# The first token tiles of a quantized feed-forward kernel, shared between two issuing queues

## What is computed

```python
hidden = jnp.concatenate([cond, cond], axis=-1)
x_mean = jnp.mean(x, axis=1, keepdims=True)
fused = jnp.concatenate([x, x_mean * ones_L, hidden[:, None, :] * ones_L], axis=-1)
relation = jax.nn.relu(jnp.einsum('bld,do->blo', fused, W) + b)

def quant_linear(x, w, b):
    xq, s_in = quant_act_uint8(x)                # one scale: max(x)/255
    wq, s_w = quant_weight_int8_perchannel(w)    # a scale for each row of w
    bq = quant_bias_int32(b, s_in, s_w)
    return jnp.einsum('btd,fd->btf', xq, wq) + bq

h = jax.nn.relu(quant_linear(relation, w1, b1))
return x + quant_linear(h, w2, b2)
```

## Time and profile before

| | before |
|---|---|
| median of the timed runs | 329.53 us (329.33 to 330.42, 3 runs) |
| the profiled execution | 330.61 us, span on the core 328.8 us |
| TensorE matmul busy | 318.3 us, 97% of the span |
| VectorE busy | 266.8 us, 81% |
| ScalarE busy | 208.9 us, 64% |
| GpSimd busy | 76.0 us, 23% |
| DMA | 75.27 MB, mean 229 GB/s |

### The profile page before, as it was taken

One profiled execution on the slowest core, in us unless ns is written; L12 is line 12 of the kernel. 1 busy time (PEld: TensorE's weight loads), 2 busy tenths in 40 slices (PEclk: granted clock), 3 DMA queues, 4 the chain that ended last, 5 costly groups with the idle time before them and its releaser, 6 DMA issues. The chain is left out here.

```text
span 328.8 us, 4649 instructions
## 1 busy us (share of the span) xinstructions
PE 318.3 (97%) x1508; PEld 181.8 (55%) x1508; DVE 266.8 (81%) x586; ACT 208.9 (64%) x335; POOL 76.0 (23%) x60
## 2 busy tenths in 40 slices
PE   6999999999999999989999999789999999999996
PEld 6888888888775544344444444334444444444444
DVE  1549988987985899999999998885759577595996
ACT  2423865587386999656666665089875958759700
POOL 1005336643500388993280000000000000000000
PEclk9999999999999999999999999999999999999999
DMA  7959999999973888747770160379953799766316
GB/s 223 272 162 255 231 166 235 251 230 359 282 153 64 81 334 335 291 173 319 324 321 0 36 222 0 127 274 388 429 203 119 275 418 426 286 237 222 143 39 255
DMA packets 49382, 75.27 MB, mean 229 GB/s; under 512 B 19768, under 2 KB 32336, under 8 KB 44624
## 3 DMA queue, kind: packets, MB, share of 16 engines
q1 hardware_dynamic: 49168, 74.72, 72.8%
q10 hardware_dynamic: 192, 0.28, 0.4%
HBM read 45.63 MB, written 25.17 MB: 215 GB/s over the span
## 5 line engine op out<-in xcount | busy, mean ns | idle before, releaser
L833 ACT ACTIVATE steps<-hidden,s_quant 128x512 int16 (+1 forms) x124 | 76.8, 710 | 21.1 <-DVE w_t L1123 11.2
L705 PE MATMUL bank<-w_t 128*128 128x512 f16 x256 | 56.3, 379 | 0.9 <-DVE w_t L1158 0.9
L1027 DVE TENSOR_SCALAR_CACHE_REDUCE hidden<-bank,qb,hmax 128x512 f32<-128x512 f32 x59 | 45.4, 807 | 5.2 <-PE bank L595 4.6
L467 PE MATMUL bank<-x_hi,cw_hi 128*128 128x512 f32 x128 | 48.3, 393 | 0.3 <-ACT x_hi L735 0.3
L467 PE MATMUL bank<-x_lo,cw_hi 128*128 128x512 f32 x128 | 48.5, 390 | 0.0
L467 PE MATMUL bank<-x_hi,cw_lo 128*128 128x512 f32 x128 | 48.4, 389 | 0.0
L1046 DVE CUSTOM_DVE_ANT_0 hidden<-hidden,bank,hmax 128x512 f32<-128x512 f32 x69 | 47.9, 742 | 0.0
L403 POOL TENSOR_TENSOR x_lo<-hidden,x_hi 128x512 fp32r<-128x512 f32 x24 | 30.4, 1300 | 54.1 <-ACT x_hi L735 54.1
L705 PEld LDWEIGHTS bank<-w_t 128*128 128x128 f16 x256 | 24.8, 98 | 31.9 <-DVE w_t L1158 1.5
L705 PE MATMUL bank<-w_t,pool_q 128*128 128x512 f16 x192 | 41.9, 379 | 0.0
L595 PE MATMUL bank<-pool_r,pool_q 128*128 128x512 f16 x152 | 38.2, 379 | 0.0
(11 more groups left out here) (132 smaller groups left out, 421.6 us busy)
## 6 DMA issues: line engine op xcount, KB each, us to landing
hidden_spill<-hidden SPq DMA_DIRECT2D x16, 1024.0 KB, 4.3
hidden<-hidden_spill SPq DMA_DIRECT2D x16, 1024.0 KB, 8.3
pool_r<-in_x_dram SPq DMA_DIRECT2D x8, 1024.0 KB, 5.3
x_in<-in_x_dram SPq DMA_DIRECT2D x28, 256.0 KB, 5.7
pool_q<-in_L_ffn_w_dram SPq DMA_DIRECT2D x7, 1024.0 KB, 9.1
out_dram<-pool_r SPq DMA_DIRECT2D x7, 1024.0 KB, 4.8
pool_r<-in_L_cond_W_dram SPq DMA_DIRECT2D x2, 1024.0 KB, 10.8
x_in<-in_x_dram SPq DMA_DIRECT2D x1, 1024.0 KB, 9.5
```

Of the source, the lines that this page charges most:

```text
L467: return pe.matmul(REL[ot][:, :], w[:, k, ot * P:(ot + 1) * P], v[:, n % 2, k, :], start=(k == 0 and w is cw_hi and v is x_hi), stop=(k == ...
L705: mm = pe.matmul(bank[TJ * par + j][:, :], hid_q[par][:, ft, j * P:(j + 1) * P], w2_t[:, ft, :], start=(ft == 0), stop=(ft == FT - 1))
L833: ins = act.activation(steps[:, q % 2, f, :], hidden[:, bass.ds(slot * HB + ft * TB, TB)], ACT.Copy, scale=s_quant[:, ft:ft + 1])
L1027: dve.tensor_scalar(hidden[:, at:at + TB], y_bank[:, :], qb1[:, ft:ft + 1], hmax[:, ft:ft + 1], ALU.add, ALU.max, accum_out=hmax[:, ft:ft ...
```

## The change

SyncE's queue issues token tiles 0 and 2 of block 0 only. ScalarE's queue issues tile 1, then weight chunk 0, then tile 3, then the three small tables as before. Destinations, sizes, semaphores and all waits stay as they are.

```diff
@@ block.sync
-            for j in range(TJ):
+            for j in range(0, TJ, 2):
                 sp.dma_start(x_in[:, 0, j * D:(j + 1) * D], x_blocks[0, :, j, :]).then_inc(x0_landed[j], 16)
             for k in range(1, KD):
                 sp.dma_start(cw_in[:, k, :], cw_turned[0, :, k, :]).then_inc(cw_landed[k], 16)
@@ block.scalar
+            act.dma_start(x_in[:, 0, D:2 * D], x_blocks[0, :, 1, :]).then_inc(x0_landed[1], 16)
             act.dma_start(cw_in[:, 0, :], cw_turned[0, :, 0, :]).then_inc(cw_landed[0], 16)
+            act.dma_start(x_in[:, 0, 3 * D:4 * D], x_blocks[0, :, 3, :]).then_inc(x0_landed[3], 16)
             act.dma_start(cond_rows, cond.rearrange("b (k p) -> b k p", p=P)).then_inc(rows_landed, 16)
```

## The result

The change makes the kernel slower: 330.53 us median (330.10 to 333.81, 19 runs) against 329.33 us (329.08 to 330.48, 19 runs); the ratio is 1.0047, 95% interval 1.0032 to 1.0063. That is +1.2 us at the medians, where -0.1 us was forecast. The time lies inside the forecast's range (328.5 to 330.9); its direction is the opposite one.

The account below looks back on a forecast made before the run. TensorE was taken as the bound from the first relation product on, so only the start mattered. Tile 1's wait going gave -0.12 us, all else 0: 329.53 - 0.12 = 329.4 us, range 328.5 to 330.9.

Parts of the forecast that it names:

- TensorE is thus the bound from the first relation product on: From the first relation product at 10.63 us TensorE has no slack; moving that product moves the end by the same amount.
- Tile 0: change 0: Token tile 0, still SyncE's first issue at 0.75 us, lands at 5.6 us as before; at most 0.74 us to gain.
- tile 0 comes sooner: Rival, faster: sharing with another piece of x brings tile 0 early, gaining at most 0.86 us, 328.7 us; chance 0.11.
- Tile 3 takes the slot of weight chunk 1, 9.0: Worst case for token tile 3 at the start: it lands at 9.0 us instead of 8.2.
- Wanted at 9.11: hidden by 0.1 us: TensorE wants token tile 3 at 9.11 us, so landing at 9.0 costs nothing, with 0.1 us to spare.
- The sum: Whole kernel: -0.12 us, from tile 1's wait going, taken from the 329.53 us median gives 329.4 us.
- Two queues are slow: Rival, slower: 216 GB/s while both queues have work, tile 3 at 10.7 us, 1.5 us lost, 331.0 us; chance 0.15.
- TensorE's clock rises later: Rival, slower: a wait for tile 3 delays TensorE's clock rise by 2 to 4 us, costing +1 to +2 us; chance 0.06.
- Issue time, the table load, the small tables: ScalarE's two extra issues of about 0.42 us delay its table load and the small tables, all covered: cost 0.

Follow-up runs that it names:

- the second profile of before: The kernel before the change, unchanged, profiled again: 329.14 us median, ratio 0.999; its profiled execution took 329.36 us.

## Why the prediction was wrong, by its own steps

- **"TensorE is thus the bound from the first relation product on"**: right. From 9.34 to 10.38 us is 1.04 us, and the span and the time grow by 1.0.
- **"Tile 0: change 0"**: wrong, in the good direction. With tile 1 and not chunk 0 beside it tile 0 lands at 4.1 us instead of 5.3 to 5.6 (and tile 1 at 4.3, not 5.8). The rival "tile 0 comes sooner" happened, and gave nothing at the median, since the last tile decides. The argument against it, that the change touches nothing beside tile 0, contradicts the prediction's own text: the neighbour is what changed.
- **"Tile 3 takes the slot of weight chunk 1, 9.0"**: right, it lands at 9.1 as the sixth piece, as its worse case had it.
- **"Wanted at 9.11: hidden by 0.1 us"**: this is the step that failed. The wanted time was read from one execution in which TensorE ran at its lower level until 9.8 us. In the second profile of before it rises near 7 us and tile 3 is wanted at 8.09; that most executions are of this kind follows from their times, not from profiles. In the changed kernel tile 3 is wanted at 7.92, where the loads of the keep-warm products end (7.66 + 0.26). Tile 3 had then no 1.0 us to spare before the change but about 0.1, and moving it from 8.0 to 9.1 costs 1.0 us in full. Even at the lower level 9.11 would not have held: the changed kernel takes up tile 0 at 4.57 instead of 5.62, and three steps of 1.17 us from there are 8.08. The wait for tile 3 was thus missed twice, by the clock and by tile 0. The sign of this was in reach: the prediction had seen the two lengths of the keep-warm products and that its execution was 1.08 us above the median, and used neither for the wanted times.
- **The sum**: -0.12 us was taken from the median, though worked out on an execution of the other kind. Against that execution it is not far off: the first relation product is 0.25 us sooner (10.38 against 10.63) and the profiled execution 0.21 us shorter. That nearness is luck, a tile 0 that came 1.5 us sooner and a tile 3 that was waited for.
- **"Two queues are slow"**: its price, 1.5 us, is near the result (and its 331.0 us lies above the range's own end, 330.9), but its mechanism, a low rate as long as both queues have work, is not what happened: they moved 380 GB/s from 6.5 to 9.5 us. What happened lies between it and the forecast. The engines are shared, but SyncE's longer queue gets two packets to each one of ScalarE's, and one chunk is slow; so the third transfer in ScalarE's queue is late. The loss is of order, not of rate.
- **"TensorE's clock rises later"**: not a later rise but a fall behind the new gap, in some executions, +1 to +3 us. The prediction named the condition, a late tile, and gave the case 0.06.
- **Issue time, the table load, the small tables**: right. The table load starts at 3.51 us and ends at 4.8, and ScalarE still waits 2.41 us for chunk 0.

What stays open: why the first strided read of the weights is slow, why a backlog on the other queue makes it slower, and why the longer queue gets the larger share of the packets. The runs exclude the stride alone, the first touch of the same places by 64 bytes, neighbouring rows in flight, and two queues as such.

## What to carry to other kernels

Read the time at which a consumer wants its data from an execution that sits at the median, or from two; a wait of nothing with "1 us to spare" may be a slower consumer and not an earlier transfer. When several transfers must all be in before work starts, ask which lands last and what has been put ahead of it or beside it: here the first one came 1.5 us sooner and the last one 1 us later, and only the last one counted. A part of a change is worth a run by itself: leaving one of the two moved tiles in its place took away the whole loss.

## What the runs showed of the hardware beyond that

- TensorE's rise from the lower to the higher level came at 7.0 and at 9.8 us in two executions of one program with nearly the same work ahead of it. Together with a tile 0 that landed 0.3 us later this makes 1.3 us at the first relation product. In eleven profiles without idle time ahead of it, the rise lies anywhere from 4.95 to 7.87 us.
- In four profiles idle time on TensorE of 1.08, 1.73, 2.00 or 2.16 us was followed by about 3.4 us at the lower level; idle times of 1.03, 1.12, 1.37, 1.46 and 1.65 us before tile 3 in five others were not. Its length alone does not decide.
- Beside another token tile, tile 0 lands at 3.9 to 4.1 us in eleven profiles and at 4.7 in one; beside the first strided chunk of the weights at 5.2 to 5.6 in four, issued within 10 ns of its neighbour each time.
- With 256 KB transfers on ScalarE's queue and more of them waiting on SyncE's, the 16 engines move 1.6 to 3.3 packets of SyncE's for each of ScalarE's third transfer, so that transfer takes 1.9 to 4.0 us from its first packet to its last (nine profiles) where it takes 0.98 us with nothing beside it.
